# Edge gathers of a graph layer: the eighth tile of every pair split over three engines, and all programs written out

## What is computed

```python
msg_in = jnp.concatenate([nodes[row], nodes[col], edge_features], axis=-1)
messages = relu(msg_in @ mW1 + mb1) @ mW2 + mb2
aggregated = jax.ops.segment_sum(messages, col, num_segments=nodes.shape[0])
upd_in = jnp.concatenate([nodes, aggregated], axis=-1)
x = _layernorm(x + relu(upd_in @ uW1 + ub1) @ uW2 + ub2, axis=-1)
```

## Time and profile before

| | |
|---|---|
| median of 3 runs | 1922.3 us (1922.01 to 1922.93) |
| the profiled execution's own time | 1922.22 us |
| its span | 1920.4 us |
| busy: PE, DVE, ACT, POOL | 74%, 80%, 65%, 75% of the span |
| chain that ended last | POOL 63%, issue 23%, PE 4%, DVE 3%, DMA 3% |
| the DMA engines' mean busy share after the first slices | 0.4 |

### The profile page before, as it was taken

The page is one execution under the profiler, slowest core; times in us unless marked ns, Lnnn a source line. Parts: engine busy times, 40 slices in busy tenths (PEclk is TensorE's granted clock), DMA queues, the critical chain, the costliest instruction groups (busy, mean ns, idle before and its releaser), DMA issues.

```text
span 1920.4 us, 56413 instructions
## 1 busy us (share of the span) xinstructions
PE 1429.3 (74%) x8716; PEld 1334.2 (69%) x8716; DVE 1540.8 (80%) x10793; ACT 1242.0 (65%) x10165; POOL 1431.4 (75%) x1527
## 2 busy tenths in 40 slices
PE   6776677777678777767768777776867878777877
PEld 6776566777667677666667667766767767766776
DVE  5568888888888888888888888888888888888883
ACT  3246766767766766766666666766666666766663
POOL 7777777777777777777777777777777777777773
PEclk8898888778877878788887887878788776877686
DMA  9664444444444444444444444444444444444441
GB/s 239 163 154 113 123 114 114 123 115 114 123 113 114 124 115 112 120 118 113 115 123 113 112 122 117 114 119 120 112 115 123 113 114 122 115 114 119 118 109 35
DMA packets 169379, 229.86 MB, mean 120 GB/s; under 512 B 98508, under 2 KB 117687, under 8 KB 168701
## 3 DMA queue, kind: packets, MB, share of 16 engines
q1 hardware_dynamic: 112484, 124.14, 23.4%
q0 software_dynamic: 48416, 97.68, 20.6%
q10 hardware_dynamic: 8254, 5.59, 1.2%
HBM read 217.59 MB, written 9.60 MB: 118 GB/s over the span
## 4 chain that ended last, share of the span: by engine, by line
POOL 63%; issue 23%; PE 4%; DVE 3%; DMA 3%; DVEq 1%; ACT 1%; POOLq 1%; SPq 1%; ACTq 0%
POOL gath L717 63%; DVE col_x L469 2%; DMA gath<-table_src,idx 1%; PE ps_sum L856 1%; DVEq L460 1%; DMA table_src<-gath 1%; PE ps_pre L824 1%; PE ps_pre L825 1%; DVE hid L1180 1%; PE ps_pre L790 0%; PE ps_pre L832 0%; POOLq L302 0%; DMA xwin<-in_xT_dram 0%; ACT hid L1000 0%; DMA col_src<-in_srcT_dram 0%
## 5 line engine op out<-in xcount | busy, mean ns | idle before, releaser
L717 POOL DMA_INDIRECT gath<-table_src,idx x1388 | 1309.6, 944 | 423.0 <-issue 420.6
L469 ACT COPY col_x<-xdeg 64x1 f32 x9428 | 912.4, 187 | 237.6 <-issue 219.6
L832 PE MATMUL ps_pre<-rhs,lhs 128*128 128x128 f32 x3226 | 603.0, 363 | 448.3 <-DVE lhs L1158 445.6
L469 DVE COPY col_x<-xdeg 64x1 f32 x9408 | 718.2, 138 | 216.0 <-issue 215.5
L832 PEld LDWEIGHTS ps_pre<-rhs,lhs 128*128 128x128 f32 x3226 | 558.8, 269 | 477.1 <-DVE lhs L1158 473.9
L856 PE MATMUL ps_sum<-onehot,hid 128*128 128x96 f32 x3322 | 473.2, 304 | 13.0 <-ACT rhs L976 11.9
L856 PEld LDWEIGHTS ps_sum<-onehot,hid 128*128 128x128 f32 x3322 | 463.3, 221 | 23.5 <-issue 15.2
L1007 ACT ACTIVATE hid<-hid 128x1024 f32<-128x1024 f32 x202 | 212.5, 1052 | 180.4 <-DVE hid L1180 177.0
L1180 DVE TENSOR_TENSOR hid<-ps_pre,gath 128x1024 f32<-128x1024 f32 x202 | 246.4, 1220 | 87.2 <-DMA gath<-table_src,idx 75.4
L1158 DVE TENSOR_SCALAR_CACHE_REDUCE lhs<-lhs,place 96x1024 f32<-96x1024 int32 x208 | 264.6, 1272 | 32.7 <-PE ps_sum L765 19.8
L1150 DVE TENSOR_TENSOR onehot<-ps_iota,dst_rel 128x768 f32<-128x768 f32 (+1 forms) x209 | 196.9, 943 | 0.1
(11 more groups left out here) (109 smaller groups left out, 639.1 us busy)
## 6 DMA issues: line engine op xcount, KB each, us to landing
lhs<-in_dst_dram SPq DMA_DIRECT2D x207, 384.0 KB
lhs<-in_edgeT_dram SPq DMA_DIRECT2D x207, 128.0 KB
gath<-table_src,idx POOLq DMA_INDIRECT x1388
table_src<-gath SPq DMA_DIRECT2D x12, 512.0 KB, 7.0
xwin<-in_xT_dram SPq DMA_DIRECT2D x208, 24.0 KB
idx<-in_srcT_dram SPq DMA_DIRECT2D x192, 4.0 KB
out_dram<-yout ACTq DMA_DIRECT2D x48, 64.0 KB, 1.6
col_src<-in_srcT_dram SPq DMA_DIRECT2D x148, 0.5 KB
```

The lines of the kernel that those rows point to most:

```text
L469: ins = copy(col_x[:, i, start + n + j:start + n + j + 1], col)
L717: pool.indirect_dma_start(gath[0:m, k, j * H:(j + 1) * H], None, table_src, src_by_tile(p, k, j, m)).then_inc(gathered[k], 16)
L832: mm = nc.tensor.matmul(to[0:m, j * H:(j + 1) * H], lhs[:, k, j * P:j * P + m], rhs[:, k, :], start=True, stop=not by_cols)
```

## The change

It has three parts.

1. Every engine's program is written out; `Fori` is gone from the pairs. Four more slots of `idx` (`AHEAD = 8`) let SP load source indices earlier.
2. From pair 13 on every pair has 7 gathers, none 8, and its last tile is split in three: 64 columns by ScalarE, 58 by VectorE (26 in one step, 32 in the next), and for the last 6 edges SP reads the node numbers into registers and issues six DMAs of one table row each into `gath`. The last 6 columns of `col_x` are zero, as is the last tile of `gath` outside those 6 rows.
3. Register work is placed otherwise. VectorE reads the addresses of four pairs' sums at once, and makes them into addresses ahead of the first batch (`place_sums`); ScalarE reads its 64 node numbers in four reads of 16, the last 32 of them a step ahead. SP also waits until the table is stored before its first step.

```diff
-PEELED = 4
-COL_K = (1, 2, 3)
-COL_FIRST = 3
+EARLY = 16
+COL_FROM = 13
 COL_TILE = PT - 1
-COL_HALF = P // 2
+COL_ACT = 64
+COL_LOAD = COL_ACT // 4
+COL_DVE = 26
+COL_ROWS = 6
+AHEAD = 2 * SLOTS
 COL_GROUP = 3
...
+        def load_regs(eng, k, start, count):
+            regs = [eng.alloc_register(f"col{next(col_regs)}") for n in range(count)]
+            for n in range(0, count, 32):
+                eng.load(regs[n:n + 32], col_src[0:1, k, start + n:start + min(n + 32, count)])
+            return regs
...
+            def load_rows(p, k):
+                sp.wait_ge(col_src_in[k], col_loads(p))
+                sp.wait_ge(hsum_made, p - SLOTS + 1)
...
+                regs = [sp.alloc_register(f"row{next(col_regs)}") for n in range(COL_ROWS)]
+                sp.load(regs, col_src[0:1, k, P - COL_ROWS:P])
+                for n, reg in enumerate(regs):
+                    src = sp.snap(reg, donate=True, min_val=0, max_val=N - 1)
+                    q = P - COL_ROWS + n
+                    sp.dma_start(gath[q:q + 1, k, COL_TILE * H:PW], table_src[bass.ds(src, 1), :]).then_inc(rows_in[k], 16)
...
             with sp.If(fit == 1):
+                stored(sp, 0)
                 pairs(sp, step, lambda *chunk: None, lambda i: None)
...
@@ ScalarE, step @@
-                copy_cols(act, nc.scalar.copy, it, k, 0, 0, cols_act)
-                copy_cols(act, nc.scalar.copy, it, k, 1, 0, cols_act)
+                if has_cols(p + 2):
+                    wait_cols(act, p + 2)
+                    first = load_regs(act, to, 0, COL_LOAD)
+                if has_cols(p + 1):
+                    copy_batch(act, nc.scalar.copy, (k + 1) % SLOTS, 2 * COL_LOAD, act_regs.pop(), cols_act)
+                if has_cols(p + 2):
+                    first += load_regs(act, to, COL_LOAD, COL_LOAD)
+                    copy_batch(act, nc.scalar.copy, to, 0, first, cols_act)
+                    act_regs.append(load_regs(act, to, 2 * COL_LOAD, COL_LOAD) + load_regs(act, to, 3 * COL_LOAD, COL_LOAD))
...
@@ VectorE, step @@
-                copy_cols(dve, nc.vector.tensor_copy, it, k, 0, COL_HALF, cols_dve)
+                if p % SLOTS == SLOTS - 1:
+                    load_starts(p - SLOTS + 1)
+                at = place_sums(p - 3) if p >= 3 else None
+                if has_cols(p + 1):
+                    to, start = (k + 1) % SLOTS, COL_ACT + COL_DVE
+                    copy_batch(dve, nc.vector.tensor_copy, to, start, load_regs(dve, to, start, P - COL_ROWS * has_rows(p + 1) - start), cols_dve)
...
-                copy_cols(dve, nc.vector.tensor_copy, it, k, 1, COL_HALF, cols_dve)
+                if has_cols(p + 2):
+                    to = (k + 2) % SLOTS
+                    wait_cols(dve, p + 2)
+                    copy_batch(dve, nc.vector.tensor_copy, to, COL_ACT, load_regs(dve, to, COL_ACT, COL_DVE), cols_dve)
```

More of the change, by code:

```diff
@@ L142, in gnn_kernel @@
         lane = sb("lane", [P, 1])
-        col_src = sb("col_src", [1, len(COL_K), P], I32)
-        col_x = sb("col_x", [D, len(COL_K), P])
+        col_src = sb("col_src", [1, SLOTS, P], I32)
+        col_x = sb("col_x", [D, SLOTS, P])
         root = sb("root", [P, 1])
@@ L236, in gnn_kernel @@
         idx_rest_in = sem("idx_rest_in")
-        idx_in = [sem(f"idx_in{i}") for i in range(SLOTS)]
+        idx_in = [sem(f"idx_in{i}") for i in range(AHEAD)]
         raw_got = [sem(f"raw_got{i}") for i in range(RAW)]
@@ L357, in steps_for_window, with pairs @@
             return p - 2
-        def pairs(eng, step, node, tail, peeled=PEELED, looped=True):
-            for it in range(peeled if looped else LAG):
+        def pairs(eng, step, node, tail):
+            for it in range(ITERS - 1):
                 for k in range(SLOTS):
                     step(it, k)
[L365 to L381, removed]
+                    if it >= LAG:
+                        for stage in STAGES[k]:
+                            node(it - LAG, stage, NP)
             def end(i, stage):
@@ L386, in end @@
                 node(c, stage, NP if c < CHUNKS else LAST, i)
-            both(ITERS - 1, ITERS - 1 - LAG)
+            for k in range(SLOTS):
+                step(ITERS - 1, k)
+                for stage in STAGES[k]:
+                    node(ITERS - 1 - LAG, stage, NP)
             end(0, UPD)
@@ L429, in gnn_kernel @@
-        col_regs = count_up()
[L431 to L457, removed]
-            regs = [eng.alloc_register(f"col{next(col_regs)}") for n in range(count)]
-            eng.load(regs, col_src[0:1, i, start:start + count])
-            for n in range(0, count, COL_GROUP):
+        def has_cols(p):
+            return COL_FROM <= p < PAIRS
@@ new lines, in col_tile, with gathers_of, got, col_loads @@
+        def col_tile(p):
+            return LAST_ROWS if is_last(p) else COL_TILE
+        def gathers_of(p):
+            return rows_of(p) if is_last(p) else PT - has_cols(p)
+        def got(p):
+            return 16 * sum(gathers_of(q) for q in range(RAW, p + 1) if q % SLOTS == p % SLOTS)
+        def col_loads(p):
+            return 16 * sum(has_cols(q) for q in range(COL_FROM, p + 1) if q % SLOTS == p % SLOTS)
+        def col_batches(p):
+            return 2 * sum(has_cols(q) for q in range(COL_FROM, p + 1))
@@ new lines, in col_before, with has_rows, rows_got @@
+        def col_before(p):
+            return next((q for q in range(p - SLOTS, COL_FROM - 1, -SLOTS) if has_cols(q)), None)
+        def has_rows(p):
+            return COL_FROM <= p < LAST_PAIR
+        def rows_got(p):
+            return 16 * COL_ROWS * sum(has_rows(q) for q in range(p % SLOTS, p + 1, SLOTS))
+        col_regs = count_up()
+        def load_regs(eng, k, start, count):
+            regs = [eng.alloc_register(f"col{next(col_regs)}") for n in range(count)]
+            for n in range(0, count, 32):
+                eng.load(regs[n:n + 32], col_src[0:1, k, start + n:start + min(n + 32, count)])
+            return regs
@@ L462, in copy_batch @@
+        def copy_batch(eng, copy, k, start, regs, done):
+            for n in range(0, len(regs), COL_GROUP):
                 of = []
@@ L468, in copy_batch, with wait_cols @@
                 for j, col in enumerate(of):
[L469 to L484, removed]
+                    ins = copy(col_x[:, k, start + n + j:start + n + j + 1], col)
+            ins.then_inc(done, 1)
+        def wait_cols(eng, p):
+            k = p % SLOTS
+            eng.wait_ge(col_src_in[k], col_loads(p))
+            if col_before(p) is not None:
+                eng.wait_ge(pe_steps, steps_for_pre(col_before(p)))
+            let(eng)
         def p_early(p):
-            return isinstance(p, int) and p < PEELED * SLOTS
+            return p < EARLY
         def src_by_tile(p, k, j, m):
-            ap = idx_all[0:m, p * PT + j:p * PT + j + 1] if p_early(p) else idx[0:m, k, j:j + 1]
+            ap = idx_all[0:m, p * PT + j:p * PT + j + 1] if p_early(p) else idx[0:m, p % AHEAD, j:j + 1]
             return bass.IndirectOffsetOnAxis(ap=ap, axis=0)
@@ L560, in load_pair, with load_idx @@
                 sp.dma_start(dst_t[0:WIN, k, 0:count], here.broadcast_to([WIN, count])).then_inc(dst_b_in[k], 16)
[L562 to L566, removed]
+            def load_idx(p):
+                if p >= EARLY + AHEAD:
+                    sp.wait_ge(hsum_made, p - AHEAD + 1)
+                sp.dma_start(idx[:, p % AHEAD, :], srcT[:, cols(p * PT, PT)]).then_inc(idx_in[p % AHEAD], 16)
             def load_window(p, it, k):
@@ L609, in step @@
                     load_pair(*pair(it, k, -PREP))
[L610 to L622, removed]
+                p = it * SLOTS + k
+                if has_cols(p + SLOTS):
+                    load_cols(p + SLOTS, col_tile(p + SLOTS), P)
@@ new lines, in step, with load_cols @@
+                if p + SLOTS == PAIRS:
+                    load_cols(p + SLOTS, TILES, TAIL)
+                if EARLY <= p + AHEAD - 1 < PAIRS:
+                    load_idx(p + AHEAD - 1)
+                if has_rows(p + PREP):
+                    load_rows(p + PREP, (k + PREP) % SLOTS)
+            def load_cols(p, tile, count):
+                if has_cols(p - SLOTS):
+                    sp.wait_ge(cols_act, col_batches(p - SLOTS))
+                    sp.wait_ge(cols_dve, col_batches(p - SLOTS))
+                of = srcT[0:count, cols(min(p, LAST_PAIR) * PT + tile, 1)].rearrange("p a -> a p")
+                sp.dma_start(col_src[:, p % SLOTS, 0:count], of, allow_slow_non_contiguous=True).then_inc(col_src_in[p % SLOTS], 16)
@@ L829, in pre @@
                 for j, m in tiles_of(p):
-                    last = [i for i, tile, count in LAST_COLS if is_last(p) and tile == j]
-                    by_cols = last or j == COL_TILE and has_cols(it, k)
+                    by_cols = has_cols(p) and (j == col_tile(p) or j == TILES and is_last(p))
                     mm = nc.tensor.matmul(to[0:m, j * H:(j + 1) * H], lhs[:, k, j * P:j * P + m], rhs[:, k, :], start=True,
```

(4 more changed lines are left out.)

123 lines of the change are left out of this document (59 added, 64 removed).

## The result

The changed kernel takes 3052.6 us (3050.16 to 3054.55, four runs); the kernel before, run beside it, 1922.15 us (1920.71 to 1922.93). The ratio is 1.588 [1.585, 1.591]: slower by 1130 us. The prediction was 2015 us, with 2073 as its high end. The sign was right, and the loss is twelve times the 93 us that were forecast. One execution of experiment 6 took 1948.7 us at a granted clock of 0.561, where the other six of that kernel have 0.76 to 0.77, and is left out of the range and ratio given there.

The account below looks back on a forecast made before the run. The prediction took POOL's gathers to bound the kernel, with VectorE 0.39 us a pair behind. VectorE's terms, +0.85, made 9.45 us a pair, +90 us; with 3 us for other parts, 1922.2 became 2015 us, range 1960 to 2073.

Parts of the forecast that it names:

- The first batch still reads 32 numbers ... +0.05: VectorE's first batch: register arithmetic goes ahead of its read, two old waits are gone; +0.05 us a pair (0 to 0.15).
- 26 take 1.72 us ... -0.10: VectorE's second batch: longer read, 26 numbers for 16, but begun earlier; -0.10 us a pair, ends -0.30 and +0.63.
- The step's four starts in one read: VectorE, one step of four: reading four sums' starts takes 0.50 us, a quarter of it a pair, +0.12.
- 9.45 us a pair: VectorE's forecast need: 8.60 plus 0.85 us, above POOL's 8.74 and the present pace of 8.99.
- the ten copies: VectorE's column copies: 58 where 48 were, +0.76 us a pair.
- With 0.15 us of arithmetic and gaps 0.65: SP's one-row DMAs at a register's address: 0.50 us each, 0.65 with arithmetic and gaps, 3.9 for six.
- The rival of 2317 us: SP becomes the bound: if a row costs 1.1 us, SP needs 11.0 us a pair; chance 0.04.
- POOL's 60 us: Gathers on POOL: 48 pairs lose their eighth gather, 48 x 1.248 = 60 us; forecast as not gained at all.
- a locked port: Rival: VectorE's ten more copies hold up POOL's gathers by at most 0.76 us a pair, 2025 us; chance 0.01.
- ScalarE's rival: ScalarE becomes the bound, needing 9.2 to 9.6 us, pace about 9.75 with TensorE waits, 2073 us; chance 0.14.

Follow-up runs that it names:

- experiment 6: Experiment 5's kernel, but every eighth pair gathers all eight tiles and builds no columns: 1903.2 us, ratio 0.991 to the kernel before.
- experiment 1: The changed kernel with VectorE's two batches swapped, 32 columns from 64 first, then 26 from 96: 2071.7 us, ratio 1.079 to the kernel before.
- experiment 5: Experiment 1's kernel with eight table rows by SP instead of six, VectorE copying 32 and 24 columns: 1931.6 us, ratio 1.007 to the kernel before.
- experiment 3: The kernel before with node numbers two places further in the row, so VectorE's and ScalarE's reads of them begin 8 bytes later: 3323.5 us, one run.

## Why the prediction was wrong

- **"The first batch still reads 32 numbers ... +0.05": the step that failed.** Measured: +5.1 us a pair. I priced a read by its count alone, 0.063 us a number, a slope through reads that all began on multiples of 16 numbers. The change moves the start to number 90, and I took the move to be free without a row that showed such a start. The rival that I would have needed stood in the text and was set aside without a chance of its own: the Trainium skill (Runtime: NRT & Kernel Launch, "Instruction fetch mechanics") gives some 200 ns a register even in bulk. For reads off the boundary the trace agrees (0.22 us a number); for reads on it, it does not (0.063). The earlier trace rows could refute the rule for their own starts only. By it the read of 32 alone would have been an estimated 6.4 us, and it took 7.14.
- **"26 take 1.72 us ... -0.10".** The read took 2.07 us, since 26 is six groups and two left over. It began 0.35 us after `turned`, as estimated (0.3), and the first copy came at 2.6 us instead of 2.2: some +0.3 in place of -0.10. The high end, +0.63, covered it. The step's four starts in one read took 0.35 us, not 0.50: four numbers from a boundary.
- **"9.45 us a pair".** With the one failed term taken out (experiment 1) the loss is 150 us where I forecast 93: (150 - 3)/195 = 0.75 us a pair over 8.99, so 9.74 for 9.45. The first copy's place came as priced (2.38 us after the addition, forecast 2.33 + 0.05), and so did the ten copies (1.96 us for 26 against 1.22 for 16, 0.74 for 0.76). The first copy of the second batch, 0.4 us later than forecast, accounts for the 0.29 and more. Part of it came back: the next addition starts 0.03 us after the last copy, 0.11 in the earlier trace rows.
- **"With 0.15 us of arithmetic and gaps 0.65" a row on SP.** The six rows take 2.35 us together, 0.4 each, so 1.5 us less than forecast; the read of six took 1.27 us, twice the 0.6 to 0.7. The two errors differ in sign, and SP needs some 0.9 us less than forecast; it was never the bound. (The read of 0.31 us for which the earlier trace rows are named there is a row of VectorE in the earlier trace rows; SP's own takes 0.27.) The rival of 2317 us fell, since a row costs 0.4 us and had to cost 0.84; the true time lay beyond 2317 us for another reason.
- **What was right:** VectorE takes the bound from POOL and POOL's 60 us are not gained. In the changed kernel the slow read alone would do that (POOL waits 1109 us for the addition), but it holds without it too: in experiment 1 POOL waits 195 us for the addition, 1.0 us a pair where 0.7 was forecast, and VectorE has 54% of the chain. Gathers stay at a mean of 943 ns (a median of 944 in the earlier trace rows), so nothing shows of a locked port. VectorE doesn't wait for gathered rows. The written-out programs, left out of the sum, are worth nothing.
- **ScalarE's rival** (9.2 to 9.6 us of its own; its terms add up to 9.4 to 9.7) is refuted by experiment 5. ScalarE's program is the same there, 64 columns and the same reads, and 195 pairs pass between the additions at 143.8 and 1917.2 us, 9.09 us a pair. So ScalarE needs at most 9.09 us, its waits for TensorE included (before the update they are 14.2 us in total there). The 9.74 us of experiment 1, the very pace that the rival named (9.75), came from VectorE. In experiment 5 ScalarE has 6% of the chain, so it is not far under that pace; its need alone was not measured.

SP's timeline in the kernel after: one pair, its rows and what follows them.
```profile
1512.27 0.35 SPq L556 DMA_DIRECT2D idx<-in_srcT_dram  x1
1514.22 2.35 SPq L630 DMA_DIRECT2D gath<-table_src  x6
1517.59 0.52 SPq L565 DMA_DIRECT2D xwin<-in_xT_dram  x1
```

TensorE's mean granted clock fell from 0.80 to 0.65 of 2.4 GHz; it was 0.73 in experiment 1 and 0.64 in experiment 3, where it waited too. In the kernel after VectorE waits for TensorE 32.6 us over the three longest such rows (13.9 in the row above), so the clock can't account for the loss.

## What to carry to other kernels

When a split of work moves the start or the count of a read into registers, work out where in the row each read begins: begin at a multiple of 16 bytes and read multiples of four 4-byte numbers; here one order of two batches was worth 981 us. A price taken from rows holds for the shapes, counts and starting addresses that these rows have; where the change leaves them, bound the term by the worst rate that any source gives, and place the new case at the high end of the range. Here the engine that had the chain and was half idle, its idle time put to "issue", was held up by its register reads; where a page looks like this, read their durations first.

## What the runs showed of the hardware

- A read into registers from an SBUF row of 4-byte numbers takes 0.25 us for each further four if its first number lies on a multiple of 16 bytes from the start of the row, else 0.22 us for each further number, to its end: as if it fetched four at a time or one at a time. The first four take 0.35 us, the first one 0.31. Starts of 0, 4, 8, 16 and 1, 2, 3, 26 were tried by themselves, on VectorE; 64, 96 (fast) and 90 (slow) in the kernels; on ScalarE shifted reads of 16 and 32 slowed down too (shortest and longest: 1.01 and 1.99 us before, 3.42 and 6.94 shifted), and on SP 6 numbers from 122 took 1.27 us and 8 from 120 took 0.53.
- Numbers left over behind the last whole group cost about 0.24 us each: 26 numbers cost 2.07 us, nearly the 2.11 of 32.
- A DMA of one table row at a register's address costs SP 0.23 us of its queue, and 0.4 us with the register work around it (2.35 us for six).
